# Four graph layers on one core: own step lists for the opening and the closing, and a new order of the steps in a round

## What is computed

```python
# 0: x @ W1.T after mixing the nodes by A_hat, batch norm over ALL tokens, relu, @ W2.T, batch norm over all tokens
# 1: h = relu(layernorm((L_norm x) @ Wc + bc)); x1 = h + x
#    4-head attention masked by adj; x2 = layernorm(x1 + o @ Wo + bo)
#    layernorm(x2 + gelu(x2 @ W1 + b1) @ W2 + b2)
# 2: h = relu(adj @ (x @ Wg0 + bg0)); h = relu(adj @ (h @ Wg1 + bg1))
#    for p in 1..4: an LSTM over windows of p nodes; its last state replaces every p-th node
# 3: graph attention: softmax(leaky_relu(s1_i + s2_j), masked) @ (x @ W)
```

## Time and profile before

| | us |
|---|---|
| median of 3 runs (lowest, highest) | 2134.87 (2134.11, 2135.21) |
| span of the profiled execution, core 0 | 2133.6 |
| first and second stage, to the first `turn_y` | 246.5 |
| opening | 111.0 |
| one round of 7 | 226.4 |
| closing | 191.3 |
| PE busy over the span | 1999.0 (94%) |
| DVE busy | 1773.5 (83%) |
| ACT busy | 1454.2 (68%) |
| POOL busy | 189.8 (9%) |

### The profile page before, as it was taken

The page is one execution under the profiler, slowest core; times in us unless marked ns, Lnnn a source line. Parts: engine busy times, 40 slices in busy tenths (PEclk is TensorE's granted clock), DMA queues, the critical chain, the costliest instruction groups (busy, mean ns, idle before and its releaser), DMA issues.

```text
span 2133.6 us, 86503 instructions
## 1 busy us (share of the span) xinstructions
PE 1999.0 (94%) x37415; PEld 1754.5 (82%) x37415; DVE 1773.5 (83%) x5049; ACT 1454.2 (68%) x4411; POOL 189.8 (9%) x252
## 2 busy tenths in 40 slices
PE   6999779999999999999999999999999999999986
PEld 3444358989898989889998989898989898899975
DVE  6779677888888988898888988888889888988855
ACT  5657336767777676767677777677776777676764
POOL 2000000010101010101010110101010001010100
PEclk9999889999999999999999999999999999999998
DMA  7847300000100001000100010001000010000000
...
DMA packets 36825, 87.84 MB, mean 41 GB/s; under 512 B 2416, under 2 KB 26992, under 8 KB 32752
## 3 DMA queue, kind: packets, MB, share of 16 engines
...
## 4 chain that ended last, share of the span: by engine, by line
PE 46%; DVE 28%; ACT 11%; issue 3%; POOL 1%; POOLq 0%; DVEq 0%; ACTq 0%
PE ps L247 13%; PE ps L249 13%; PE ps L248 13%; DVE stats L1574 4%; ACT pool_mem L1450 3%; DVE hl_a L1626 2%; DVE pool_mem L1728 2%; PE ps L1190 2%; DVE pool_mem L1715 2%; DVE t L1595 1%; DVE pool_mem L1709 1%; DVE mv L1578 1%; DVE pool_mem L1713 1%; PE ps L261 1%; DVE t L1605 1%
## 5 line engine op out<-in xcount | busy, mean ns | idle before, releaser
L1450 ACT ACTIVATE pool_mem<-ps,lstm_b 128x64 f32<-128x64 f32 (+2 forms) x2496 | 607.7, 353 | 120.8 <-PE ps L249 113.6
L247 PE MATMUL ps<-hl_a,w_hi 128*128 128x64 f16 (+2 forms) x3776 | 542.1, 214 | 25.8 <-DVE hl_a L618 16.0
L248 PE MATMUL ps<-hl_a,w_hi 128*128 128x64 f16 (+2 forms) x3776 | 541.0, 214 | 0.0
L249 PE MATMUL ps<-hl_a,w_lo 128*128 128x64 f16 (+2 forms) x3776 | 540.8, 214 | 0.0
L247 PEld LDWEIGHTS ps<-hl_a,w_hi 128*128 128x128 f16 x3776 | 349.1, 97 | 60.8 <-DVE hl_a L618 17.1
L247 PE MATMUL ps<-hl_b,w_hi 128*128 128x84 f16 (+2 forms) x2112 | 368.3, 229 | 5.0 <-DVE hl_b L1739 3.4
L248 PE MATMUL ps<-hl_b,w_hi 128*128 128x84 f16 (+2 forms) x2112 | 368.9, 229 | 0.0
L249 PEld LDWEIGHTS ps<-hl_a,w_lo 128*128 128x128 f16 x3776 | 349.0, 97 | 23.8 <-issue 2.0
L249 PE MATMUL ps<-hl_b,w_lo 128*128 128x84 f16 (+2 forms) x2112 | 367.5, 229 | 0.0
L248 PEld LDWEIGHTS ps<-hl_a,w_hi 128*128 128x128 f16 x3776 | 349.1, 97 | 20.7 <-issue 1.4
L247 PE MATMUL ps<-pool_mem,w_hi 128*128 128x64 f16 (+2 forms) x3072 | 352.0, 200 | 2.4 <-DVE pool_mem L1733 1.3
...
## 6 DMA issues: line engine op xcount, KB each, us to landing
...
```

The costliest lines, as they stand in the source:

```text
L247: nc.tensor.matmul(o, l[0], r[0], start=first, stop=False, skip_group_check=True)
L248: nc.tensor.matmul(o, l[0], r[1], start=False, stop=False, skip_group_check=True)
L249: return nc.tensor.matmul(o, l[1], r[0], start=False, stop=last, skip_group_check=True)
L1450: op = nc.scalar.activation(gates[s][h][:, g, m * w:(m + 1) * w], gate_place(s, h, g, m, w), ACT.Tanh, bias=lstm_b[:, bias:bias + 1], scal ...
```

## The change

`OPENING` (85 entries) and `CLOSING` (197) are lists of their own; `opening()` and `closing()` return them, with tile 1 and tile 8. `ROUND` keeps its 282 entries in another order. Which entries are in a list stays the same everywhere; no instruction differs.

```diff
--- before.py
+++ after.py
@@ -76,46 +76,82 @@
 
 
 ROUND = """
-1:cheb.1 0:pack3.1 0:cell3.0 1:conv.1 0:hid3.0 1:v.0 0:inp4.1 1:norm_g1.1 0:cell4.1 0:pack3.0 1:q.0 1:k.0 1:xa_bias.1
-1:turn_x1.1 0:inp4.0 0:cell4.0 1:scores.0 1:v.1 1:exps.0 0:hid4.0 1:q.1 1:k.1 0:inp5.0 0:hid4.1 1:scores.1 1:exps.1
-0:inp5.1 0:cell5.1 0:cell5.0 1:turn_probs.1 0:hid5.1 1:turn_probs.0 0:inp6.1 1:attend.1 0:hid5.0 0:cell6.1
-1:attn_out.1 0:hid6.1 1:attend.0 0:inp6.0 1:norm_g2.1 0:pack4.1 0:cell6.0 1:turn_x2.1 0:inp7.1 0:cell7.1 0:hid6.0
-0:hid7.1 0:pack4.0 1:attn_out.0 1:mlp_up.1 1:gelu_split.1 1:norm_g2.0 0:inp8.1 0:cell8.1 0:hid8.1 0:inp7.0 0:cell7.0
-1:mlp_down.1 1:turn_x2.0 0:inp9.1 0:cell9.1 0:hid7.0 1:norm_g3.1 0:inp8.0 1:mlp_up.0 1:gelu_split.0 1:norm_l1.1
-0:hid9.1 0:inp10.1 0:cell8.0 1:mlp_down.0 1:mix0.1 0:cell10.1 0:hid8.0 0:hid10.1 0:inp9.0 1:norm_g3.0 1:gcn0.1
-0:cell9.0 1:mix1.1 1:norm_l1.0 0:hid9.0 0:inp10.0 0:turn_state.1 1:gcn1.1 1:mix0.0 0:norm_l2.1 0:cell10.0 0:hid10.0
-1:inp0.1 0:turn_xc.1 0:turn_state.0 1:cell0.1 1:gcn0.0 0:gat.1 0:gat_keys.1 1:mix1.0 1:hid0.1 0:gat_exps.1 1:inp1.1
-1:cell1.1 0:norm_l2.0 1:hid1.1 0:turn_att.1 1:gcn1.0 0:turn_xc.0 0+norm_y 0:gat_mix.1 1:inp0.0 1:cell0.0 0:norm_l3.1
-0:gat.0 0+turn_y.1 0:gat_keys.0 1:inp2.1 1:cell2.1 0+norm_l0.1 1:hid0.0 1:inp1.0 0:gat_exps.0 1:hid2.1 0:turn_att.0
-0:gat_mix.0 1:cell1.0 0+cheb.1 1:inp3.1 1:hid1.0 0:norm_l3.0 0+conv.1 0+turn_y.0 1:cell3.1 0+norm_l0.0 0+norm_g1.1
-1:inp2.0 1:cell2.0 0+cheb.0 0+xa_bias.1 1:hid2.0 1:inp3.0 0+conv.0 0+turn_x1.1 0+norm_g1.0 1:cell3.0 0+v.1 0+q.1
-0+xa_bias.0 1:hid3.1 0+turn_x1.0 1:hid3.0 0+k.1 0+scores.1 1:pack3.0 0+v.0 0+exps.1 1:pack3.1 0+q.0 0+k.0 1:inp4.0
-1:cell4.0 1:hid4.0 0+turn_probs.1 1:inp4.1 0+scores.0 0+attend.1 1:cell4.1 0+exps.0 1:inp5.0 1:cell5.0 1:hid5.0
-0+attn_out.1 0+norm_g2.1 0+turn_probs.0 1:inp6.0 1:cell6.0 0+attend.0 1:hid6.0 1:hid4.1 1:inp5.1 0+turn_x2.1 1:pack4.0
-0+attn_out.0 0+norm_g2.0 0+mlp_up.1 0+gelu_split.1 1:inp7.0 1:cell7.0 1:hid7.0 1:cell5.1 0+turn_x2.0 0+mlp_down.1
-1:hid5.1 0+norm_g3.1 1:inp6.1 0+mlp_up.0 0+gelu_split.0 1:inp8.0 0+norm_l1.1 1:cell6.1 1:cell8.0 1:hid6.1 1:hid8.0
-0+mlp_down.0 1:pack4.1 0+mix0.1 1:inp9.0 1:cell9.0 1:inp7.1 1:cell7.1 1:hid9.0 1:inp10.0 1:hid7.1 1:inp8.1 0+norm_g3.0
-1:cell10.0 1:cell8.1 1:hid10.0 1:hid8.1 0+gcn0.1 0+norm_l1.0 1:inp9.1 1:turn_state.0 1+norm_y 1:cell9.1 1:norm_l2.0
-1:hid9.1 0+mix0.0 0+mix1.1 1:inp10.1 1:turn_xc.0 1:cell10.1 1:hid10.1 0+gcn0.0 1:gat.0 1:gat_keys.0 0+mix1.0
-1:turn_state.1 1:gat_exps.0 0+gcn1.1 1:norm_l2.1 1:turn_att.0 0+gcn1.0 1:gat_mix.0 1:turn_xc.1 0+inp0.1 0+cell0.1
-1:norm_l3.0 1+turn_y.0 0+inp0.0 0+cell0.0 1:gat.1 1+norm_l0.0 0+hid0.1 0+hid0.0 0+inp1.1 0+cell1.1 1+cheb.0 0+hid1.1
-1:gat_keys.1 0+inp1.0 0+cell1.0 1+conv.0 1:gat_exps.1 0+inp2.1 0+hid1.0 1:turn_att.1 0+cell2.1 1:gat_mix.1 0+hid2.1
-0+inp3.1 0+inp2.0 1:norm_l3.1 1+norm_g1.0 0+cell2.0 1+turn_y.1 0+cell3.1 1+norm_l0.1 0+hid2.0 0+inp3.0 0+hid3.1
-1+xa_bias.0 1+turn_x1.0
+1:cheb.1 0:pack3.1 0:cell3.0 1:conv.1 1:v.0 1:q.0 1:norm_g1.1 0:hid3.0 1:k.0 1:xa_bias.1 0:inp4.1 0:pack3.0
+1:turn_x1.1 0+norm_y 1:scores.0 0:inp4.0 0:cell4.0 1:v.1 0:cell4.1 0:hid4.0 1:q.1 0:hid4.1 1:k.1 0:inp5.0 1:scores.1
+0:inp5.1 1:exps.0 1:exps.1 0:cell5.0 0:cell5.1 1:turn_probs.0 0:hid5.1 1:turn_probs.1 0:hid5.0 0:inp6.1 1:attend.1
+1:attend.0 0:cell6.1 1:attn_out.1 0:hid6.1 1:norm_g2.1 0:pack4.1 0:inp6.0 0:cell6.0 1:turn_x2.1 0:inp7.1 0:hid6.0
+0:cell7.1 0:pack4.0 0:hid7.1 1:attn_out.0 1:mlp_up.1 1:gelu_split.1 1:norm_g2.0 0:inp8.1 0:inp7.0 0:cell8.1
+1:mlp_down.1 0:hid8.1 0:cell7.0 1:turn_x2.0 0:hid7.0 1:norm_g3.1 0:inp9.1 0:inp8.0 0:cell9.1 1:mlp_up.0 1:gelu_split.0
+1:norm_l1.1 0:cell8.0 0:hid9.1 0:hid8.0 0:inp10.1 1:mlp_down.0 1:mix0.1 0:inp9.0 1:norm_g3.0 0:cell10.1 0:cell9.0
+1:gcn0.1 1:norm_l1.0 0:hid10.1 1:mix1.1 0:hid9.0 0:inp10.0 0:turn_state.1 1:gcn1.1 0:norm_l2.1 0:cell10.0 1:mix0.0
+0:hid10.0 1:inp0.1 0:turn_xc.1 1:cell0.1 1:gcn0.0 0:gat.1 0:gat_keys.1 1:mix1.0 0:turn_state.0 1:hid0.1 1:inp1.1
+0:gat_exps.1 0:norm_l2.0 1:gcn1.0 0:turn_att.1 1:cell1.1 0:gat_mix.1 0:turn_xc.0 1:hid1.1 1:inp0.0 1:cell0.0
+0:norm_l3.1 0:gat.0 0+turn_y.1 0:gat_keys.0 1:inp2.1 1:cell2.1 0+norm_l0.1 1:hid0.0 0:gat_exps.0 1:hid2.1 1:inp1.0
+0:turn_att.0 0+cheb.1 1:cell1.0 0:gat_mix.0 1:hid1.0 0:norm_l3.0 1:inp3.1 0+conv.1 0+turn_y.0 1:cell3.1 1:inp2.0
+0+norm_l0.0 1:cell2.0 0+norm_g1.1 0+cheb.0 1:hid2.0 1:inp3.0 0+xa_bias.1 0+turn_x1.1 0+conv.0 0+norm_g1.0 1:cell3.0
+0+xa_bias.0 0+v.1 0+q.1 0+k.1 0+turn_x1.0 1:hid3.0 0+scores.1 1:hid3.1 1:pack3.0 0+v.0 0+exps.1 0+q.0 0+k.0 1:pack3.1
+1:inp4.0 1:cell4.0 0+scores.0 0+turn_probs.1 1:hid4.0 1:inp4.1 0+attend.1 1:inp5.0 0+exps.0 1:cell4.1 1:cell5.0
+1:hid4.1 1:hid5.0 0+attn_out.1 1:inp6.0 0+norm_g2.1 0+turn_probs.0 1:cell6.0 0+attend.0 1:hid6.0 1:inp5.1 0+turn_x2.1
+0+attn_out.0 1:pack4.0 0+norm_g2.0 0+mlp_up.1 0+gelu_split.1 1:cell5.1 1:inp7.0 0+turn_x2.0 1:hid5.1 1:cell7.0
+0+mlp_down.1 1:hid7.0 1:inp6.1 0+mlp_up.0 1:inp8.0 0+norm_g3.1 0+gelu_split.0 0+norm_l1.1 1:cell8.0 1:cell6.1 1:hid8.0
+1:hid6.1 0+mlp_down.0 1:pack4.1 1:inp9.0 1:cell9.0 0+mix0.1 1:hid9.0 1:inp7.1 1:cell7.1 1:hid7.1 1:inp10.0 0+norm_g3.0
+1:inp8.1 1+norm_y 1:cell10.0 1:cell8.1 1:hid10.0 1:hid8.1 0+gcn0.1 1:inp9.1 1:turn_state.0 0+norm_l1.0 1:cell9.1
+1:norm_l2.0 1:hid9.1 0+mix1.1 1:inp10.1 1:turn_xc.0 0+mix0.0 1:cell10.1 1:gat.0 1:hid10.1 1:gat_keys.0 0+gcn0.0
+1:turn_state.1 1:gat_exps.0 1:norm_l2.1 0+gcn1.1 1:turn_att.0 0+mix1.0 1:gat_mix.0 1:turn_xc.1 0+gcn1.0 1:norm_l3.0
+0+inp0.1 1+turn_y.0 0+cell0.1 0+inp0.0 0+cell0.0 1+norm_l0.0 0+hid0.1 1:gat.1 0+hid0.0 0+inp1.1 0+cell1.1 1+cheb.0
+0+hid1.1 1:gat_keys.1 0+inp1.0 0+cell1.0 1+conv.0 0+inp2.1 0+hid1.0 1:gat_exps.1 1:turn_att.1 0+cell2.1 1:gat_mix.1
+0+inp2.0 0+hid2.1 1:norm_l3.1 1+norm_g1.0 0+cell2.0 0+inp3.1 1+turn_y.1 0+cell3.1 1+norm_l0.1 0+hid2.0 0+hid3.1
+1+xa_bias.0 1+turn_x1.0 0+inp3.0
 """.split()
 ROUND = [(int(entry[0]), int(entry[1] == "+"), entry[2:]) for entry in ROUND]
 
 
+OPENING = """
+0+norm_y 0+turn_y.1 0+norm_l0.1 1+norm_y 0+turn_y.0 0+cheb.1 0+norm_l0.0 0+conv.1 0+norm_g1.1 0+cheb.0 0+xa_bias.1
+0+turn_x1.1 0+conv.0 0+v.1 0+q.1 0+norm_g1.0 0+xa_bias.0 0+k.1 0+turn_x1.0 0+scores.1 1+turn_y.0 0+v.0 0+exps.1 0+q.0
+0+k.0 0+scores.0 0+turn_probs.1 0+attend.1 0+exps.0 0+attn_out.1 0+norm_g2.1 0+turn_probs.0 0+attend.0 1+norm_l0.0
+0+turn_x2.1 0+attn_out.0 0+norm_g2.0 0+mlp_up.1 0+gelu_split.1 1+cheb.0 0+turn_x2.0 0+mlp_down.1 0+norm_g3.1
+0+mlp_up.0 0+gelu_split.0 1+conv.0 0+norm_l1.1 0+mlp_down.0 0+mix0.1 0+gcn0.1 0+norm_g3.0 0+norm_l1.0 0+mix1.1
+0+mix0.0 1+norm_g1.0 0+gcn1.1 1+xa_bias.0 0+gcn0.0 0+mix1.0 0+inp0.1 0+cell0.1 0+hid0.1 0+gcn1.0 0+inp1.1 0+cell1.1
+0+inp0.0 0+hid1.1 0+cell0.0 1+turn_y.1 0+hid0.0 1+turn_x1.0 0+inp2.1 0+cell2.1 0+inp1.0 0+cell1.0 0+hid1.0 1+norm_l0.1
+0+hid2.1 0+inp3.1 0+inp2.0 0+cell2.0 0+cell3.1 0+hid2.0 0+hid3.1 0+inp3.0
+""".split()
+CLOSING = """
+1:cheb.1 0:pack3.1 0:cell3.0 1:conv.1 1:v.0 1:norm_g1.1 0:inp4.1 0:hid3.0 0:cell4.1 1:xa_bias.1 1:q.0 1:k.0
+1:turn_x1.1 0:hid4.1 0:inp5.1 1:scores.0 0:pack3.0 1:v.1 0:cell5.1 1:exps.0 1:q.1 1:k.1 0:hid5.1 0:inp4.0 1:scores.1
+0:cell4.0 1:exps.1 0:inp6.1 0:cell6.1 1:turn_probs.0 0:hid6.1 0:hid4.0 1:turn_probs.1 0:pack4.1 0:inp5.0 1:attend.1
+0:cell5.0 1:attn_out.1 0:hid5.0 1:attend.0 0:inp7.1 0:inp6.0 1:norm_g2.1 0:cell7.1 0:cell6.0 1:turn_x2.1 0:hid6.0
+1:attn_out.0 0:hid7.1 1:norm_g2.0 0:pack4.0 1:mlp_up.1 0:inp8.1 1:gelu_split.1 0:cell8.1 1:turn_x2.0 0:inp7.0
+1:mlp_down.1 0:hid8.1 1:mlp_up.0 1:norm_g3.1 1:gelu_split.0 0:cell7.0 0:inp9.1 0:cell9.1 0:hid7.0 1:norm_l1.1 0:inp8.0
+0:hid9.1 1:mlp_down.0 1:mix0.1 1:norm_g3.0 0:inp10.1 0:cell8.0 1:gcn0.1 1:norm_l1.0 0:hid8.0 0:cell10.1 0:inp9.0
+1:mix0.0 1:mix1.1 0:cell9.0 1:gcn0.0 1:mix1.0 0:hid10.1 1:gcn1.1 0:hid9.0 1:gcn1.0 0:turn_state.1 1:inp0.1 1:cell0.1
+1:inp0.0 1:hid0.1 1:cell0.0 1:inp1.1 0:inp10.0 1:cell1.1 1:hid1.1 0:norm_l2.1 1:hid0.0 0:cell10.0 1:inp2.1 1:cell2.1
+1:inp1.0 1:cell1.0 1:hid1.0 1:hid2.1 1:inp3.1 0:turn_xc.1 1:inp2.0 0:hid10.0 1:cell2.0 1:hid2.0 1:cell3.1 1:hid3.1
+1:inp3.0 1:pack3.1 1:cell3.0 1:hid3.0 0:gat.1 1:pack3.0 0:turn_state.0 1:inp4.1 1:cell4.1 1:inp4.0 0:gat_keys.1
+1:cell4.0 1:hid4.0 0:norm_l2.0 1:hid4.1 1:inp5.1 1:inp5.0 0:gat_exps.1 1:cell5.0 1:hid5.0 1:cell5.1 1:hid5.1 1:inp6.0
+1:cell6.0 1:hid6.0 0:turn_xc.0 1:inp6.1 1:pack4.0 1:cell6.1 1:inp7.0 1:cell7.0 1:hid6.1 1:hid7.0 0:gat.0 1:inp8.0
+1:pack4.1 0:gat_keys.0 1:inp7.1 1:cell7.1 1:hid7.1 1:cell8.0 1:inp8.1 1:hid8.0 1:cell8.1 1:inp9.0 1:hid8.1 1:cell9.0
+0:gat_exps.0 1:hid9.0 1:inp9.1 1:cell9.1 1:inp10.0 1:hid9.1 1:cell10.0 1:inp10.1 1:hid10.0 1:turn_state.0 1:cell10.1
+1:hid10.1 1:norm_l2.0 0:turn_att.1 1:turn_state.1 1:turn_xc.0 0:gat_mix.1 0:turn_att.0 1:gat.0 1:norm_l2.1
+1:gat_keys.0 1:turn_xc.1 0:gat_mix.0 1:gat_exps.0 1:gat.1 1:gat_keys.1 1:turn_att.0 1:gat_mix.0 1:gat_exps.1
+1:turn_att.1 0:norm_l3.0 0:norm_l3.1 1:gat_mix.1 1:norm_l3.0 1:norm_l3.1
+""".split()
+
+
+def steps_of(order):
```

(7 more changed lines are left out.)

## The result

The changed kernel takes **2095.73 us** (median of 4 runs, 2091.76 to 2096.32) where the kernel before takes 2135.04 on the same chip: ratio 0.9819, interval 0.9807 to 0.983. One of the four executions of the kernel before took 3943.05 us; the ratio is formed without it. That is 39 us less. The forecast was 2113 (2098 to 2127): the right sign, but 17 us too high and outside its range. The profiled execution took 2096.32 us, span 2094.5.

A forecast was written before the change was run, and what follows sets the result against it. It took PE as the busiest engine (94% of the span), with order able to change only waits: span 2133.6 - 11 (opening) + 0 (rounds) - 11 (closing) = 2111.6, against the median 2113 us, range 2098 to 2127.

The forecast's parts named there:

- The replay: Opening: following which engine waits for whom in the new list, seam reached 11.6 us earlier, taken as -11.
- none in the opening: Opening: no gain counted from matmuls leaving the half clock, since waits of 1 to 3 us remain.
- only 6.7 us can be won there by any order: Round: PE is busy 219.7 of 226.4 us at full clock, so only the remaining 6.7 could be won.
- the list of pairs: Round: producer-consumer pairs whose PE cover changes; old waits gone -2.2, new ones +2.3 to +2.6, so 0 per round.
- `mix1.1` +0.7: Round: `1:mix1.1` follows `1:gcn0.1` at once and needs ScalarE's copy, a new wait of 0.7 us.
- Rival 1: Rounds: new waits are hidden and old ones gone, -2.2 in each of seven, -15 us, total 2098; chance 0.16.
- the term -9.0: Closing to the end of `1:cell10.1`: PE waits shrink from 17.5 to 8.5 us, a gain of 9.0.
- The tally: Closing: sum over producer-consumer pairs of chain need less PE work between, where positive; 17.5 us before, 8.5 in the new list.
- +1.2: Final chain: stream 0's two `gat_mix` sums on DVE among stream 1's cost 1.2 us more; chain replayed at 28.
- Rival 2: Opening and closing give half, -5 and -6 us, total 2124; chance 0.17.
- rival 3: Rounds lose at the exponentials, DVE work ahead of `0:cell6.1`: up to 4.9 us a round, total 2147; chance 0.05.
- Rival 4: Opening stays at 1.2 GHz throughout, 19 us more instead of 11 less, total 2143; chance 0.02.

The follow-up runs named there:

- open_warm: The changed kernel with 59 matmuls whose result nobody reads, at 14 places of the opening: 2088.83 us, 0.9789 of the kernel before.
- tail_bare: The changed kernel with stream 0's last attention steps moved out of the final chain, back between stream 1's cells: 0.9874 of the kernel before.
- tail_warm: The kernel before with 17 matmuls whose result nobody reads, in three waits of the final chain: 0.9991 of the kernel before.

## Why the prediction came out wrong

- **Opening, right in its times, wrong in its bound.** The replay gave `turn_x1.1` 260.8, `mix0.1` 308.7, `inp0.1` 322; the trace has 259.46, 306.91 and 320.31, 1.3 to 1.8 earlier, of which 1.5 are the untouched start. The stage lost 12.6 us; the replay had 11.6, and -11 was taken. But "none in the opening" of the clock was a wrong sentence: it rose from 0.82 to 0.88, and 5.7 us more were to be had at 0.98 (open_warm). The replay kept PE's steps at the lengths they had at the low level.
- **Rounds, the failed step is "only 6.7 us can be won there by any order".** It takes the idle time in the profile for all that PE waits. By start times PE waited 9.9 us a round, and the list of pairs had no term for the 3.3 us of it that are booked as busy. The pairs were read well: `mix1.1` +0.7 (0.78), `gat_mix.1` +0.5 (1.22 in the list with its `gcn1.0` in front, larger), `1:turn_xc.0` +0.8 (0.55), the wait before `1+turn_y.0` gone, in all 0 (+0.09). The round still lost 0.9, in PE's busy time (-0.99): three waits fewer and eight short ones fewer, -1.0. Rival 1 had the direction, with 15 us and for another reason: the new waits that it took as hidden did come.
- **Closing, the term -9.0, the largest miss.** The tally was trusted to 10% since it met the 16 us of before. It overstated the new list's shortfalls: 8.5 against 3.1 us (146.60 less 143.51 at full clock). The needs that I put into it, which the prediction does not list, came from stretches where DVE and ACT were loaded: 5.0 us from `cell3` to `inp4` and from `cell6` to `inp7`, 4.5 from `cell5` to `cell6`. The trace of before shows 3.40, 3.3 and 2.77 in the closing itself, so that its total met the trace there was luck: some other shortfalls must have been too low, and which is not known. What is over the full-clock work went from 16.0 to 3.1, -12.9 where -9.0 was forecast. The full-clock work itself went from 148.5 to 143.5, -5.0 where 3.3 was moved; the other 1.7 is known to some 0.8 only, since the clock of before is given as 0.98. It may well be of the kind seen in the rounds: PE stops 21 times before and 6 times after, which at 0.16 is an estimate of 2.4.
- **Final chain, +1.2 against -0.9.** The two `gat_mix` sums of stream 0 found room in the waits, as tail_bare shows: without them the chain is no shorter (27.8 against 25.9, part of which is its clock of 0.62). With their products among them PE's clock is at 0.81 where it was 0.74, worth up to 1.0 (tail_warm).
- **The rest.** Rival 2 (the ends give half) and rival 3 (rounds lose at the exponentials) fell: `scores.1` waits 0.34 us, and `cell6.1` has no wait of its own in the list. Rival 4 fell with 0.88. Of the 17 us between forecast and result 6 are the rounds, 5.6 the closing's tally, 2.1 the final chain, 1.6 the opening and 1.5 the untouched stages.
